# The denominator's 1e-8 added by a one-row matmul, and one masked product with a difference of value blocks in place of two

## The reference

```python
dist = jnp.sqrt((diff * diff * m_h).sum(axis=-1) + 1e-08)
dist = jnp.where(mask[None], dist, jnp.inf)
neg_d, loc = jax.lax.top_k(-dist, K)
...
infl = jnp.exp(-topd)
infl = infl / (infl.sum(axis=-1, keepdims=True) + 1e-08)
neighbor_v = v_h[batch_ix, top_idx]
context = jnp.einsum('btk,btkd->btd', infl, neighbor_v)
```

## Time and profile before

| | |
|---|---|
| median of 3 runs | 686.34 us |
| profiled execution, its own time | 686.94 us |
| its span | 685.2 us |
| VectorE busy | 602.9 us (88% of the span) |
| TensorE matmuls busy | 615.5 us (90%) |
| ScalarE busy | 519.2 us (76%) |
| POOL busy | 488.4 us (71%) |

### The profile page before, as it was taken

The page is one execution under the profiler, slowest core; times in us unless marked ns, Lnnn a source line. Parts: engine busy times, 40 slices in busy tenths (PEclk is TensorE's granted clock), DMA queues, the critical chain, the costliest instruction groups (busy, mean ns, idle before and its releaser), DMA issues. The chain is left out here.

```text
span 685.2 us, 22680 instructions
## 1 busy us (share of the span) xinstructions
PE 615.5 (90%) x6050; PEld 432.1 (63%) x6114; DVE 602.9 (88%) x4954; ACT 519.2 (76%) x1574; POOL 488.4 (71%) x717
## 2 busy tenths in 40 slices
PE   4997887899999999999999999999999999999876
PEld 2543444566776676666666666666666666667654
DVE  4895458899999999999999999999999999999860
ACT  2896125688888888888888888888888888888752
POOL 3111314788888888888888888888888888888662
PEclk9998566899999999999999999999999999999999
DMA  7220000000001010001010101010001000000000
GB/s 212 77 77 5 10 9 20 16 22 27 23 27 28 26 28 27 27 27 28 27 27 26 28 26 28 26 28 26 27 27 28 26 24 28 27 26 25 18 12 16
DMA packets 41183, 21.22 MB, mean 31 GB/s; under 512 B 6040, under 2 KB 40544, under 8 KB 41056
## 3 DMA queue, kind: packets, MB, share of 16 engines
q1 hardware_dynamic: 41056, 19.77, 10.1%
HBM read 10.44 MB, written 4.19 MB: 21 GB/s over the span
## 5 line engine op out<-in xcount | busy, mean ns | idle before, releaser
L1009 DVE MAX8 top<-modn_all 128x8 f32<-128x32 f32 x2048 | 207.1, 175 | 6.4
L562 POOL TENSOR_TENSOR big<-big,con 128x512 f32<-128x512 f32 x128 | 160.4, 1275 | 22.4 <-DVE big L1068 22.4
L1015 DVE MATCH_REPLACE8 modn_all<-top,modn_all 128x32 f32<-128x32 f32 x1024 | 166.4, 173 | 0.0
L1260 PE MATMUL psC<-vst,big 128*128 128x68 f32 x512 | 103.0, 283 | 9.7 <-POOL big L562 7.7
L502 POOL TENSOR_TENSOR wmod_sb<-key,meet 128x512 f32<-128x512 f32 x64 | 67.8, 1060 | 51.8 <-DVE meet L1096 51.8
L1261 PE MATMUL psC<-vst,big 128*128 128x68 f32 x512 | 99.7, 276 | 0.0
L1260 PEld LDWEIGHTS psC<-vst,big 128*128 128x128 f32 x512 | 78.3, 193 | 31.4 <-POOL big L562 30.6
L1261 PEld LDWEIGHTS psC<-vst,big 128*128 128x128 f32 x512 | 78.7, 194 | 0.0
L1015 DVE MATCH_VALUE_LOAD modn_all<-top,modn_all 128x8 f32 x1024 | 77.3, 75 | 0.0
L771 ACT ACTIVATE psD<-key 128x256 f32<-128x256 f32 x64 | 24.8, 388 | 51.0 <-issue 47.7
L1286 PE MATMUL psW<-sqs,selm 128*16 128x192 f32 x256 | 55.9, 343 | 2.8 <-POOL sqs L512 2.8
(11 more groups left out here) (215 smaller groups left out, 1578.4 us busy)
## 6 DMA issues: line engine op xcount, KB each, us to landing
tst<-qT_all SPq DMA_DIRECT2D x256, 17.0 KB
big<-in_x SPq DMA_DIRECT2D x16, 256.0 KB, 2.8
xs<-in_x SPq DMA_DIRECT2D x64, 64.0 KB, 1.9
out<-yo SPq DMA_DIRECT2D x64, 64.0 KB, 1.6
sst<-nst SPq DMA_DIRECT2D x128, 3.0 KB
tst<-nst SPq DMA_DIRECT2D x128, 2.0 KB
con<-in_consts SPq DMA_DIRECT2D x1, 581.5 KB, 6.8
wmod_sb<-in_wmod SPq DMA_DIRECT2D x1, 384.0 KB, 5.8
```

The costliest lines, as they stand in the source:

```text
L562: nc.gpsimd.tensor_tensor(wab[:, k % 2, v].rearrange("p (r t) -> p r t", r=4), wsel.rearrange("p (r t) -> p r t", r=4), part.unsqueeze(1). ...
L1009: last = v.max(top[:, u, h, where], low_high[:, u, h])
L1015: last = v.match_replace(low_high[:, u, h], top[:, u, h, 1:9], low_high[:, u, h], GONE)
L1260: mm(o, wab[:, k % 2, 0, cols], vst[:, blk + 1:blk + 3, r], start=True, stop=False)
```

## The change

The masked product with `of_before` goes. With w the selected weights, `own` the mask, V_own and V_before the values, w·own·V_own + w·before·V_before is written as w·V_before + (w·own)·(V_own − V_before), as the two masks add up to one. VectorE writes the selection straight into `wab[.., 0]`, POOL makes the one product and, ahead of it, the difference of the value blocks (`vdif`, 272 elements a partition). The first four matmuls wait only for the selection, the other four for the product and the difference. VectorE's add of 1e-8 goes, and a matmul with one contraction row (a one times 1e-8, 128 columns of weights, 16 columns of data) adds it in `psC` at the end; `c_ready` moves to it.

```diff
@@ -49,7 +49,8 @@
 C_SELE = C_SELQ + NR * HD
 C_BLK = C_SELE + HD
 C_EXP = C_BLK + NG * NR
-C_END = C_EXP + NE * ER
+C_TINY = C_EXP + NE * ER
+C_END = C_TINY + 1
 
 
 def constants():
@@ -80,6 +81,7 @@
         c[h * RANK:(h + 1) * RANK, C_BLK + (h % NG) * NR + h // NG] = 1.0
     for x in range(NE):
         c[x, C_EXP + x * ER:C_EXP + (x + 1) * ER] = 1.0
+    c[0, C_TINY] = 1e-8
     return c
 
 
@@ -188,12 +190,11 @@
         fst = sb("fst", [P, 2, 4 * CH], BF16)
         infl = z8_all[:, 0:8 * CH].rearrange("p (s x) -> p s x", s=2)
         wab = big[:, 0].rearrange("p s (v x) -> p s v x", v=2)
-        wsel = big[:, 1, 0, 0:4 * CH]
         count_f = big[:, 1, 1, 0:2 * P]
         vst = sb("vst", [P, NBLK, 4, VP])
+        vdif = sb("vdif", [P, 2, 2, 4, VP])
         qh = sb("qh", [P, 4, NH, 2 * HD])
         cst = sb("cst", [P, 2, NH, VD])
-        den = sb("den", [P, 2, NH])
         rden = sb("rden", [P, 2, NH])
         n2 = sb("n2", [P, 2, 4 * NH])
         lnn = sb("lnn", [P, 4 * NH])
@@ -230,6 +231,7 @@
         pDT, pZ = psW[:, 1], psW[:, 1]
         pHigh = psW[:, 1, 0:NH * NT]
         pC = psC[:, 0:8 * VP]
+        pDen = pC.rearrange("p (n x) -> p n x", x=VD)[:, :, HD]
         pN = psW[0:2 * NH, 0, 3 * WIN:6 * WIN]
         pNN = psW[:, 0, 6 * WIN:6 * WIN + NH]
         pN2 = psX[:, 0:P]
@@ -323,12 +325,12 @@
         root_done = sem("root_done")
         infl_ready = sem("infl_ready")
         w_ready = sem("w_ready")
+        vdif_ready = sem("vdif_ready")
         wab_ready = sem("wab_ready")
         v_ready = sem("v_ready")
         vst_ready = sem("vst_ready")
         c_ready = sem("c_ready")
         cst_ready = sem("cst_ready")
-        den_done = sem("den_done")
         rden_ready = sem("rden_ready")
         hsc_ready = sem("hsc_ready")
         mix_step = sem("mix_step")
@@ -556,12 +558,15 @@
 
                 k = i - 1
                 if there(k):
+                    blk = 2 * (k % CPB)
+                    pool.wait_ge(vst_ready, 2 * k + 2)
+                    need(pool, c_ready, k - 1)
+                    nc.gpsimd.tensor_tensor(vdif[:, k % 2], vst[:, blk + 1:blk + 3], vst[:, blk:blk + 2],
+                                            ALU.subtract).then_inc(vdif_ready, 1)
                     pool.wait_ge(w_ready, k + 1)
-                    need(pool, c_ready, k - 1)
-                    for v, part in enumerate((of_own, of_before)):
-                        nc.gpsimd.tensor_tensor(wab[:, k % 2, v].rearrange("p (r t) -> p r t", r=4),
-                                                wsel.rearrange("p (r t) -> p r t", r=4),
-                                                part.unsqueeze(1).broadcast_to([P, 4, CH]), ALU.mult).then_inc(wab_ready, 1)
+                    nc.gpsimd.tensor_tensor(wab[:, k % 2, 1].rearrange("p (r t) -> p r t", r=4),
+                                            wab[:, k % 2, 0].rearrange("p (r t) -> p r t", r=4),
+                                            of_own.unsqueeze(1).broadcast_to([P, 4, CH]), ALU.mult).then_inc(wab_ready, 1)
 
             def routing(i):
                 if i == 0:
@@ -1038,13 +1043,6 @@
                     if i == 1:
                         expert_matrices(1)
 
-                k = i - 2
-                if there(k):
-                    s = k % 2
-                    dve.wait_ge(cst_ready, 2 * k + 2)
-                    need(dve, rden_ready, k - 1)
-                    v.tensor_scalar(den[:, s], cst[:, s, :, HD], 1e-8, None, ALU.add).then_inc(den_done, 1)
-
                 k = i + 1
                 if there(k):
                     dve.wait_ge(outer_ready, k + 1)
@@ -1053,8 +1051,8 @@
 
                 k = i - 2
                 if there(k):
-                    dve.wait_ge(den_done, k + 1)
-                    v.reciprocal(rden[:, k % 2], den[:, k % 2]).then_inc(rden_ready, 1)
+                    dve.wait_ge(cst_ready, 2 * k + 2)
+                    v.reciprocal(rden[:, k % 2], cst[:, k % 2, :, HD]).then_inc(rden_ready, 1)
 
                 if there(i):
                     dve.wait_ge(picked, 6 * i + 2)
@@ -1064,8 +1062,8 @@
                 if there(k):
                     dve.wait_ge(count_ready, k + 1)
                     dve.wait_ge(infl_ready, k + 1)
-                    need(dve, wab_ready, 2 * k)
-                    v.scalar_tensor_tensor(out=wsel, in0=pZ, scalar=KEEP, in1=infl[:, k % 2], op0=ALU.is_ge,
+                    need(dve, c_ready, k - 1)
+                    v.scalar_tensor_tensor(out=wab[:, k % 2, 0], in0=pZ, scalar=KEEP, in1=infl[:, k % 2], op0=ALU.is_ge,
                                            op1=ALU.mult).then_inc(w_ready, 1)
 
                 if there(i):
@@ -1253,12 +1251,22 @@
                     pe.wait_ge(vst_ready, 2 * k + 2)
                     need(pe, cst_ready, 2 * k)
                     keep_clock(psC, PW, {NCH: 0, NCH + 1: 9}.get(i, 3))
-                    pe.wait_ge(wab_ready, 2 * k + 2)
-                    for r in range(4):
-                        cols = slice(r * P, (r + 1) * P)
-                        o = pC[:, r * 2 * VP:(r + 1) * 2 * VP].rearrange("p (v x) -> p v x", v=2)
-                        mm(o, wab[:, k % 2, 0, cols], vst[:, blk + 1:blk + 3, r], start=True, stop=False)
-                        last = mm(o, wab[:, k % 2, 1, cols], vst[:, blk:blk + 2, r], start=False, stop=True)
+                    def context(part, values, first):
+
+                        for r in range(4):
+                            o = pC[:, r * 2 * VP:(r + 1) * 2 * VP].rearrange("p (v x) -> p v x", v=2)
+                            done = mm(o, wab[:, k % 2, part, r * P:(r + 1) * P], values[:, :, r], start=first and r == 0,
+                                      stop=not first, skip_group_check=True)
+                        return done
+
+                    pe.wait_ge(w_ready, k + 1)
+                    context(0, vst[:, blk:blk + 2], True)
+                    pe.wait_ge(vdif_ready, k + 1)
+                    pe.wait_ge(wab_ready, k + 1)
+                    last = context(1, vdif[:, k % 2], False)
+                    last = mm(pDen, con[0:1, C_ID:C_ID + 1].broadcast_to([1, P]),
+                              con[0:1, C_TINY:C_TINY + 1].broadcast_to([1, 4 * NG * 2]), start=False, stop=True,
+                              skip_group_check=True)
                     last.then_inc(c_ready, 1)
 
                 k = i - 1
```

## The result

| | before | after |
|---|---|---|
| median of 4 runs (lowest to highest), us | 686.24 (685.01 to 686.57) | 700.25 (698.31 to 702.60) |
| profiled execution: time, span, granted clock | 686.94, 685.2, 0.960 | 702.60, 700.8, 0.946 |

The ratio is 1.0209 [1.0175, 1.0243]: slower, as forecast, but 14 us slower where 4.5 were forecast, and past the end of the range. Six more runs of the same kernel in a later experiment lay between 690.19 and 702.86. The median of all ten is 698.8, and I measure the miss against that.

The account below looks back on a forecast made before the run. ScalarE's delivery to each scan, through a loop across engines, was taken as the bound. Short steps 2.5, three-block steps 0.8 and ends 1.2 made +4.5 us: median 690.8, own range 688.6 to 693, with rivals (b) and (c) 684.8 to 695.8.

Parts of the forecast that it names:

- C: The context matmuls on TensorE, 16 records; forecast to start 0.16 us before the scan and end 2.16 after.
- The gap of 0.07: On TensorE, a matmul record of another geometry starts only 0.07 us before the previous one ends.
- the pair of 0.38: The one-row matmul's two records on TensorE, taken as 0.38 us, lengthening C by 0.31 after 0.07 of overlay.
- the sum's first two terms: Steady steps: 28 short steps at 0.09 us more, 2.5; seven steps with three projected blocks at 0.12, 0.8.
- its cover: On POOL, the product behind the subtraction is ready 1.7 us before C's second half needs it; the subtraction costs nothing.
- rival (a): VectorE is the bound, so dropping its add saves up to 18 us: 668 us; chance 0.04.
- Rival (b): The small matmul's records lie over C without the gap, some 0.2 us (deciding price 0.22): 685.7 us; chance 0.18.
- Rival (c): TensorE becomes the bound; a further 0.1 us in 42 steps is paid in full: 695.3 us; chance 0.13.
- The sign named for it: In the profile after, steps near 8.84 us and TensorE without idle time before the counting matmul at L1299.
- Rival (d): POOL still holds C back, so 42 steps pay about 0.3 us each: 699 us; chance 0.02.
- the term for the ends: At the start and in the drain, `cst` waited openly for C four times: 4 x 0.31 = 1.2 us more.

Follow-up runs that it names:

- The first experiment: The changed kernel without the one-row matmul, the 1e-8 added on VectorE again: 685.95 us, ratio 0.9967 to the kernel before.
- the 128-row form: The changed kernel with the 1e-8 added by a matmul of 128 contraction rows (identity weights) instead of one row: 686.53 us, ratio 1.0004 to the kernel before.
- the ends alone: The changed kernel with the one-row matmul only for the first six and last six chunks, the 1e-8 left out between: 691.01 us.
- no add: The changed kernel with neither the one-row matmul nor VectorE's add, the 1e-8 left out: 684.84 us, ratio 0.9983 to the kernel before.
- the middle alone: The changed kernel with the one-row matmul only for chunks 6 to 57, the 1e-8 left out in the others: 690.28 us.
- The kernel with no add and the signs first: The changed kernel with the 1e-8 left out and ScalarE's `cst` copy behind the two sign copies: 669.35 us, ratio 0.9742 to the kernel before.

## Why the prediction was right and wrong

**Right: the path and the price.** Each step began when ScalarE delivered, before and after: every scan starts 0.03 us after its copy. C was forecast to start 0.16 before the scan and end at 2.16 after it; it started at -0.15 and ended at 2.17. The gap of 0.07, the pair of 0.38 (0.39), `cst` 2.19 after the scan (2.20) and the transposes without overlay came as they were read from the earlier trace rows. The short steps became 8.75 where 8.73 was forecast, and the step with three projected blocks 8.88 where 8.86 comes out of 8.74 + 0.12. In all 3.9 us against the 3.3 of the sum's first two terms.

**Right: what cost nothing.** The subtraction took 0.76 us (0.6 estimated, 1.06 the bound) and its cover held; the product alone takes 1.27. The first experiment shows the factored product free, even 1.2 better. VectorE's add, counted at nothing, is worth 0.7 us over 57 steps; rival (a) had given 18. Rival (b) needed a price under 0.22: the one-row pair costs 0.32 on the chain, and the 128-row form, at 0.17, falls on the other side of that point and takes the 8.64 that (b) described. Rival (c) was right that TensorE's stream has no slack left: the step with twelve projection matmuls pays their 0.12 in full. It was wrong that more would come on top, as the short steps are 8.75 and not 8.84. The sign named for it, no idle time before the counting matmul, doesn't decide: that matmul waits 0.16 in both kinds of step, behind the load of its weights. Rival (d) had 699, near what was measured, but that is chance: C started 0.15 before the scan and no longer waited for POOL.

**Wrong: the term for the ends.** The step that failed is "Outside the pattern `cst` waited openly for C four times ... 4 x 0.31 = 1.2". It prices twelve matmuls in the filling and emptying pipeline as four waits at full clock, and takes the granted clock as it was. Measured, those waits alone grew by 3.7 us (8.6 against 4.9, alike in both profiles). The ends cost 6.2 us with the middle left alone, and about 9 in the changed kernel (698.8 - 686 - 3.9). In the opening TensorE stays at 1.2 GHz for 21 us with the ends alone, for 28 and 34 in the two profiles of the changed kernel, against 17; there TensorE is busy for most of the time and works at half its speed, so it is the bound. The drain is smaller: with ScalarE's order as it was, what follows the last scan took 24.2 to 26.3 us in the profiles with the one-row matmul there, 23.4 to 24.4 in those without it. Rows that said so were at hand: the page's clock strip showed half clock at the start, and the windows of the opening showed TensorE busy 38.70 of 45 us. The sum needed a range for the length of that stretch, and I gave none.

**How far this is shown.** That the loss in the ends comes from the one-row matmul is shown by the kernels with it there alone and without it anywhere. That the time at 1.2 GHz carries most of it is supported by the profiles, by the keepers, which take 5.7 us back and leave the steady part as it is, and by the clock listed for every run. Its median is 0.962 in the kernel before, 0.961 with no add, 0.960 with the middle alone, 0.956 with the first two chunks, 0.953 with the ends alone, 0.950 in the changed kernel and 0.962 in that one with more keepers. Worked out as above, that is 52 us at 1.2 GHz in a run before and 70 after; within the 86 runs of the kernel before and within the ten of the changed one, a microsecond more of it goes with 0.4 and 0.5 us more of time. So the 18 us are worth some 7 to 9, an estimate that meets the 9 of the ends. It doesn't account for all: the changed kernel with more keepers has the clock of the kernel before and is still some 3 us above 686 + 3.9, with the time of the twelve keepers in it. Two profiles fit less well. The kernel with 128 rows, with a steady part near that of no add, had its profiled execution (691.21) with a stretch of 34 us, though 8 of its ten runs lay at or under 687.2. The kernel with no add and the signs first had 27 us in its profile (675.67), the slowest of its five. So the stretch varies from run to run without any one-row matmul, and the one-row matmul makes the long form common. Why the clock then stays low, whether for the gaps on both sides of the pair or for something else, stays open. Of the 4.0 us by which the first scan came later in the profiled execution nothing is the change's: no context matmul has run by then, the second profile of the same kernel has that scan at 104.4, and over all the kernels it lay anywhere from 103 to 109 us.

## What to carry to other kernels

Price a small matmul by its geometry: padded to the 128 rows of its neighbours it was laid over them, and with one row it was not. Price the filling and the emptying of a pipeline apart from its steady part, with the clock granted there as a term with a range of its own. And when an operation moves off an engine's queue, look for the order that it had enforced: the gain found here lay in ScalarE's order, which the add on VectorE had tied down where it stood.

## What the runs showed that I had not expected

- Matmuls can be added for a gain. Six more clock-keeping matmuls in each of two steps made the changed kernel 5.7 us faster (693.1 against 698.8), and two of three taken away in the steady part cost nothing in clock there (steady 496.6 against 501.9).
- Two one-row matmuls in the first two chunks cost about 3 us (688.09 against 684.84, medians of ten runs), though each is a pair of 0.39 us at 2.4 GHz.
- More rows were cheaper than fewer. A float32 sum over 128 rows, with 128 times the products, lengthened C by 0.17 us, the same sum over one row by 0.32. The Trainium skill, TensorEngine Tiling (Array Packing), Tiling Modes, says that a change of tiling mode drains TensorE; the trace agrees as far as the overlay goes, with a next record that starts 0.07 before the end of the one ahead instead of 0.17, and shows the same when only the contraction rows change.
